# A two-layer mixture kernel on one core: routing arithmetic in fewer instructions, another split table, extra products in two gaps

## What is computed

```python
# layer 0: per-sample LoRA mixture, then a layer norm and a ternary, fake-quantised product
y = x @ W_base.T + b_base + 2.0 * einsum(x, As, Bs, cond_8)
xn = (y - mean(y)) * rsqrt(var(y) + 1e-5) * gamma + beta
xq = round(xn / s) * s,            s = max|xn| / 127        # over the whole tensor
wq = alpha * sign(w) * (|w| > d),  d = 0.7 * mean|w|, alpha = sum(|w| mask) / sum(mask)
x  = x + xq @ wq.T
# layer 1: the two best of 8 experts per sample and a shared MLP, then a 4-bit quantised FFN
w, sel = top_k(softmax(cond_8), 2);  w = w / sum(w)
c  = sum over sel of w * mlp_e(x) + mlp_shared(x)           # mlp: (gelu(x@g) * (x@u)) @ d
x  = x + ffn(c)                                             # scales are maxima over whole tensors
```

## Time and profile before

| | us |
|---|---|
| median of 3 runs (lowest, highest) | 471.18 (466.37, 471.56) |
| the profiled execution's own time | 469.8 |
| its span | 468.1 |
| end of stage one (last maximum of a chunk) | 66.5 |
| first expert product | 99.5 |

### The profile page before, as it was taken

One profiled execution on the slowest core, in us unless ns is written; L12 is line 12 of the kernel. 1 busy time (PEld: TensorE's weight loads), 2 busy tenths in 40 slices (PEclk: granted clock), 3 DMA queues, 4 the chain that ended last, 5 costly groups with the idle time before them and its releaser, 6 DMA issues.

```text
span 468.1 us, 8624 instructions
## 1 busy us (share of the span) xinstructions
PE 393.8 (84%) x2602; PEld 346.6 (74%) x2602; DVE 334.8 (72%) x571; ACT 270.3 (58%) x406; POOL 252.8 (54%) x444
## 2 busy tenths in 40 slices
PE   5998987989999999999999999999999960000697
PEld 4675855779999999999999998877767640000497
DVE  4286648857888777767777766736958899979662
ACT  3355578855454545454545454676657899568360
POOL 1266644777777666666565401555457025969230
PEclk9997999999999999999999999999999995555599
DMA  8679870058777776767777721900000000000012
GB/s 277 239 265 340 307 242 0 1 215 272 269 233 260 246 275 235 267 239 268 234 259 249 251 78 26 355 2 1 1 0 0 1 0 0 0 1 0 0 73 109
DMA packets 31651, 71.28 MB, mean 152 GB/s; under 512 B 3571, under 2 KB 19702, under 8 KB 26614
## 3 DMA queue, kind: packets, MB, share of 16 engines
q1 hardware_dynamic: 28982, 66.33, 40.6%
q0 software_dynamic: 1152, 4.19, 2.4%
q10 hardware_dynamic: 1472, 0.20, 0.3%
HBM read 55.12 MB, written 15.60 MB: 151 GB/s over the span
## 4 chain that ended last, share of the span: by engine, by line
PE 65%; DVE 15%; POOL 7%; ACT 7%; issue 2%; DMA 2%; POOLq 1%; SPq 0%; ACTq 0%; DVEq 0%
PE ps L180 47%; PE ps L758 11%; DVE S L198 9%; PE ps L761 4%; DVE G L189 3%; PE ps L177 2%; POOL U_i L192 1%; DMA wbr<-in_L_cond_W_base_dram 1%; ACT ps L186 1%; POOL t_i L192 1%; POOL Hl L189 1%; ACT xnT L186 1%; DMA wscr<-wst 1%; POOL XCh L192 1%; ACT sq L186 1%
## 5 line engine op out<-in xcount | busy, mean ns | idle before, releaser
L713 POOL CAST xg<-XT 128x64 fp32r x312 | 113.8, 411 | 56.2 <-PE ps L180 50.2
L180 PE MATMUL ps<-xg,Wr 128*128 128x256 f32 x936 | 120.1, 284 | 1.1 <-POOL xg L713 1.1
L186 ACT ACTIVATE Gb<-ps 128x512 f32<-128x512 f32 x110 | 65.8, 598 | 94.8 <-PE ps L180 94.7
L189 DVE TENSOR_TENSOR HbS<-Gb,ps 128x512 f32<-128x512 f32 x110 | 75.4, 686 | 59.0 <-PE ps L180 57.1
L180 PEld LDWEIGHTS ps<-xg,Wr 128*128 128x128 f32 x936 | 114.2, 190 | 1.5 <-POOL xg L713 1.5
L186 ACT ACTIVATE Hh<-HbS 128x512 fp32r<-128x512 f32 x110 | 69.0, 628 | 12.9 <-DVE HbS L189 12.6
L758 PE MATMUL ps<-WD,Hh 128*128 x312 | 74.3, 328 | 0.0
L761 PE MATMUL ps<-WD,Hl 128*128 x312 | 69.4, 223 | 0.0
L189 DVE TENSOR_TENSOR Hl<-HbS,Hh 128x512 fp32r<-128x512 f32 x92 | 65.8, 723 | 2.5
L761 PEld LDWEIGHTS ps<-WD,Hl 128*128 128x128 f32 x312 | 59.8, 192 | 0.0
L758 PEld LDWEIGHTS ps<-WD,Hh 128*128 128x128 f32 x312 | 59.0, 189 | 0.0
(11 more groups left out here) (187 smaller groups left out, 699.7 us busy)
## 6 DMA issues: line engine op xcount, KB each, us to landing
Wr<-wscr SPq DMA_DIRECT2D x39, 1024.0 KB, 5.0
wscr<-wst SPq DMA_DIRECT2D x16, 512.0 KB, 4.7
yscr<-Yb SPq DMA_DIRECT2D x39, 128.0 KB, 2.7
stg<-n_L_cond_skill_gate_dram SPq DMA_DIRECT2D x8, 256.0 KB, 6.2
stg<-in_L_cond_skill_up_dram SPq DMA_DIRECT2D x8, 256.0 KB, 6.5
wdr<-n_L_cond_skill_down_dram SPq DMA_DIRECT2D x8, 256.0 KB, 5.8
out_dram<-X SPq DMA_DIRECT2D x7, 256.0 KB, 2.0
X<-in_x_dram SPq DMA_DIRECT2D x3, 512.0 KB, 6.5
```

Source lines behind the costliest of these rows:

```text
L180: return lambda e: e.matmul(o_, l, r, start=start, stop=stop, skip_group_check=True)
L186: return lambda e: e.activation(o_, i_, func, **kw)
L189: return lambda e: e.tensor_tensor(o_, a, b, op)
L713: k_xg[i] = pool.do(lambda e, s=s: e.tensor_copy(xg[:, i % XR, :, T * s:T * s + T], XT[:, :, :, bass.ds(regb[i][s], 1)].rearrange("p a t o ...
```

## The change

There are three parts. In `route()`, the running sum over experts becomes one `tensor_tensor_scan`, the seven comparisons that build `etF` one wide comparison and a reduction, two multiplications one, the four index writes one, and the ternary mask with its two sums four instead of eight. That makes 9 VectorE instructions of 29; they do not leave the places in the rounds where `fill` puts them. Second, `SPLITS` takes two tiles instead of three in rounds 3 and 4, and three instead of two in rounds 6 and 7. Third, two groups of products are added whose results nobody reads: eight of `ones` by `ones` ahead of everything on TensorE, for which the memset of `ones` moves ahead of that of `identF` on POOL, and ten of `AsTh` by `xTh` in round 2, between `hidden(1)` and `rows()`.

```diff
--- before.py
+++ after.py
@@ -137,6 +137,7 @@
         bcI = at("bcI", [128, 1], I32)
         bcF = at("bcF", [128, 1], F32)
         etF = at("etF", [1, 40], F32)
+        etX = at("etX", [1, NT, E - 1], F32)
         ST = at("ST", [128, 2, 8], F32)
         KC = at("KC", [128, 8], F32)
         assert off[0] <= RH
@@ -252,8 +253,8 @@
             load_w(n)
 
 
+        k_one = pool.do(lambda e: e.memset(ones[:, :], 1.0))
         pool.do(lambda e: e.memset(identF[:, :], 0.0))
-        pool.do(lambda e: e.memset(ones[:, :], 1.0))
         k_io8 = pool.do(lambda e: e.iota(ioi[:, :], pattern=[[1, NSLOT]], base=0, channel_multiplier=0))
         k_bc = pool.do(lambda e: e.iota(bcI[:, :], pattern=[[0, 1]], base=0, channel_multiplier=1))
         k0 = pool.do(lambda e: e.memset(tri[:, :], 1.0))
@@ -339,29 +340,25 @@
             d_f = dve.do(red(S[:, 10:11], fwr[:, :], ADD, True), l_fw)
             d_ = dve.do(ts(S[:, 80:88], S[:, 80:88], RM, RM, ADD, SUB), d_)
             yield
-            d_ = dve.do(cp(S[:, 88:96], S[:, 80:88]), d_)
-            yield
-            for i in range(1, E):
-                d_ = dve.do(tt(S[:, 88 + i:89 + i], S[:, 87 + i:88 + i], S[:, 88 + i:89 + i], ADD), d_)
-                yield
+            d_ = dve.do(lambda e: e.tensor_tensor_scan(S[:, 88:96], ones[:, 0:8], S[:, 80:88], 0.0, MUL, ADD), d_, k_one)
+            yield
             d_ = dve.do(tt(S[:, 96:104], S[:, 88:96], S[:, 80:88], SUB), d_)
-            d5 = dve.do(ts(etF[:, 0:NT], iof[0:1, 0:NT], S[0:1, 88:89], None, ALU.is_ge))
+            d5 = dve.do(tt(etX[0:1, :, :], iof[0:1, 0:NT].rearrange("p (i a) -> p i a", a=1).broadcast_to([1, NT, E - 1]),
+                           S[0:1, 88:95].rearrange("p (a e) -> p a e", a=1).broadcast_to([1, NT, E - 1]), ALU.is_ge))
             yield
             d_ = dve.do(stt(S[:, 96:104], S[:, 96:104], float(SL), S[:, 72:80], MUL, ADD), d_)
+            d5 = dve.do(red(etF[:, 0:NT].rearrange("p (i a) -> p i a", a=1), etX[0:1, :, :], ADD), d5)
             yield True
             p_f = pe.do(mm(bank[6][:, 16:17], ones[:, :], S[:, 10:11], True, True), d_f)
-            for i in range(1, E - 1):
-                yield
-                d5 = dve.do(stt(etF[:, 0:NT], iof[0:1, 0:NT], S[0:1, 88 + i:89 + i], etF[:, 0:NT], ALU.is_ge, ADD), d5)
-                if i < 3:
-                    k = 48 if i == 1 else 56
-                    d_ = dve.do(tt(S[:, k:k + 8], S[:, k:k + 8], S[:, 96:104], MUL), d_)
-                if i == 3:
-                    d_ = dve.do(red(S[:, 42:44].rearrange("p (k a) -> p k a", a=1),
-                                    S[:, 48:64].rearrange("p (k e) -> p k e", k=2), ADD), d_)
-                if i == 4:
-                    for p in range(4):
-                        tok["sidx"] = dve.do(ts(sidx[:, 2 * p:2 * p + 2], S[:, 42:44], 4.0, float(p), MUL, ADD), d_)
+            yield
+            two = S[:, 48:64].rearrange("p (k e) -> p k e", k=2)
+            d_ = dve.do(tt(two, two, S[:, 96:104].rearrange("p (a e) -> p a e", a=1).broadcast_to([128, 2, E]), MUL), d_)
+            yield
+            d_ = dve.do(red(S[:, 42:44].rearrange("p (k a) -> p k a", a=1), two, ADD), d_)
+            yield
+            tok["sidx"] = dve.do(stt(sidx[:, :].rearrange("p (q k) -> p q k", k=2),
+                                     S[:, 42:44].rearrange("p (a k) -> p a k", a=1).broadcast_to([128, 4, 2]), 4.0,
+                                     iof[:, 0:4].rearrange("p (q a) -> p q a", a=1).broadcast_to([128, 4, 2]), MUL, ADD), d_)
             yield
             dve.do(ts(tmpP[:, :], iof[:, :], S[:, 42:43], None, ALU.is_equal), d_)
             dve.do(ts(etI[:, 0, 0:NT], etF[:, 0:NT], 512.0, None, MUL), d5)
@@ -372,20 +369,15 @@
             yield
             d_ = dve.do(ts(S[:, 44:45], bank[6][:, 16:17], 0.7 / 16384, None, MUL), p_f)
             yield
-            d6 = dve.do(ts(S[:, 45:46], S[:, 44:45], -1.0, None, MUL), d_)
-            dve.do(ts(tpos[:, :], fwr[:, :], S[:, 44:45], None, ALU.is_gt), d_)
-            yield
-            d_ = dve.do(ts(tneg[:, :], fwr[:, :], S[:, 45:46], None, ALU.is_lt), d6)
+            d6 = dve.do(ts(tneg[:, :], fwr[:, :], -1.0, S[:, 44:45], MUL, ALU.is_gt), d_)
+            yield
+            d_ = dve.do(stt(tpos[:, :], fwr[:, :], S[:, 44:45], tneg[:, :], ALU.is_gt, SUB), d6)
             yield True
             p_ = pe.do(mm(bank[6][0:1, 0:NSLOT], bcF[:, :], Pm[:, :], True, True), d_P)
-            d7 = dve.do(tt(tsc[:, :], tpos[:, :], tneg[:, :], ADD), d_)
-            d_ = dve.do(tt(tpos[:, :], tpos[:, :], tneg[:, :], SUB), d_)
-            yield
-            d7 = dve.do(red(S[:, 46:47], tsc[:, :], ADD), d7)
-            yield
-            d_ = dve.do(tt(tsc[:, :], tpos[:, :], fwr[:, :], MUL), d7)
-            yield
-            d_ = dve.do(red(S[:, 47:48], tsc[:, :], ADD), d_)
+            dve.do(red(S[:, 46:47], tpos[:, :], ADD, True), d_)
+            yield
+            d_ = dve.do(lambda e: e.tensor_tensor_reduce(out=tsc[:, :], in0=tpos[:, :], in1=fwr[:, :], scale=1.0, scalar=0.0,
+                                                         op0=MUL, op1=ADD, accum_out=S[:, 47:48]), d_)
             yield True
             tok["ord"] = dve.do(cp(ordI[:, :], bank[6][0:1, 0:NSLOT]), p_)
             yield True
@@ -410,6 +402,8 @@
                 if not held:
                     held = bool(next(routing, True))
 
+        for _ in range(8):
+            pe.do(mm(bank[3][:, 0:128], ones[:, :], ones[:, :], True, True), k_one, sig=False)
         fill(1)
         A0, A1, AZ, AV, AR = (bank[0], bank[1]), bank[2], bank[3], bank[4], (bank[5], bank[7])
         a_xh, d_xl, d_hs, p_h, p_z, p_v, p_r = {}, {}, {}, {}, {}, {}, {}
@@ -450,7 +444,7 @@
                 a_sq[i] = act.do(acp(sq[:, i % 2, :], AZ, ACT.Square, bias=KC[:, 5:6]), p_z[i], *opt(p_v, i - 2))
                 a_zg[i] = act.do(acp(xnT[:, cols(i)], AZ, ACT.Identity, scale=S[:, 8:9], bias=KC[:, 6:7]), p_z[i], tok["gb"])
 
-        SPLITS = (0, 2, 2, 3, 3, 2, 2, 2, 0, 3, 0, 0)
+        SPLITS = (0, 2, 2, 2, 2, 2, 3, 3, 0, 3, 0, 0)
         for n in range(12):
             i, held = n, False
             if i < 8:
@@ -472,6 +466,8 @@
                 a_be[i] = act.do(acp(xnT[:, cols(i)], xnT[:, cols(i)], ACT.Identity, bias=S[:, 9:10]), d_xn[i])
             if n == 2:
                 hidden(1)
+                for _ in range(10):
+                    pe.do(mm(AZ, AsTh[:, :], xTh[:, 0, :], True, True), sig=False)
                 rows()
             if n >= 2:
                 norm_in(n - 2)
```

## The result

The changed kernel takes 467.32 us (median of 20 runs, 465.87 to 470.16) where the kernel before takes 470.36 (20 runs, 466.07 to 472.43) beside it on the same chip. The ratio is 0.995, with a 95% interval of 0.9926 to 0.9973: a gain of 3.0 us by the medians and 2.4 by the ratio, real but about a third of the 8.7 forecast.

A forecast was written before the change was run, and what follows sets the result against it. It took TensorE's chain (65%) as the bound, slowed in stage one by the low clock before 24 us and a pause at 36. Terms 5.3 + 3.5 - 0.1 = 8.7 us off 471.18 gave 462.5, range 457.5 to 468.0.

The forecast's parts named there:

- The splits: Rounds 5 and 6: moving third tiles removes 6.0 us excess, less one 0.74 wait; net 5.3 us, bounds 0 and 6.0.
- That the clock stays high: Rounds 6 and 7: TensorE's clock stays high after the new third tiles' wait, as in round 4; no loss charged.
- the slower rival: Ten products return nothing, full transfer queue delays `sq` in rounds 6 and 7, clock falls: 475.6 us, chance 0.05.
- The ten products: Round 2: cost 2.3 us at the high clock, give back 5.8 through round 3; net 3.5, bounds -4.3 and 4.5.
- the rival in which the clock rises late: Rounds 1 to 3: the ten start low and rise on the way, gaining 0.8 instead of 3.5: 465.2 us, chance 0.20.
- The eight products: TensorE's start: they run at the low level, mostly covered by the wait for `wbr`; loss 0.1 us, at most 0.6.
- The routing at nothing: VectorE in stage one: shorter routing arithmetic hides behind other work; gain 0, bounds 0 and 1.0 us.
- The cover named: Stage one rounds: TensorE's own work in a round hides VectorE's routing operations, so their saving counts 0.
- The sum itself: Whole kernel: splits 5.3, ten products 3.5 and eight products -0.1 add to 8.7 us.
- what stage one gives or loses should pass to the end undiminished: Stage one to the end: later stages start from its results, so all 8.7 us should reach the total.
- "both": Stage one: clock rises late and transfers set the pace, 0.8 + 3.0 - 0.1 = 3.7 us gained: 467.5 us, chance 0.10.
- its transfers: Rounds 4 to 8: transfers set the pace, 2.3 us longer; ScalarE waits in each of rounds 5 to 8; 464.8, chance 0.13.

The follow-up runs named there:

- halved transfers: Changed kernel sending only the high half of each expert weight to the scratch tensor (256 KB a tile), read twice, so remainders are wrong: 467.36 us, ratio 0.9978.
- late `WQ`: Changed kernel with the three `WQ` loads issued at the end of round 8 instead of round 4: 467.02 us, ratio 0.9965.
- the even table: Changed kernel with `SPLITS` at two tiles in each of rounds 1 to 8, three in round 9: 462.12 us, ratio 0.9889.
- the even table once more: Changed kernel with two tiles in each of rounds 1 to 8, run again in another group: 462.13 us, ratio 0.9866.
- the even table alone: Kernel before with only `SPLITS` set to two tiles in each of rounds 1 to 8, old routing, no added products: 466.73 us, ratio 0.9941.

## Why the prediction was wrong

**The splits: the step that failed.** The prediction wrote "I charge one wait as in round 3, 0.74, since four buffers still stand between, and leave the clock high", and gave the term 5.3 us. In the profile, what lies behind the start of round 5 is worth 2.7, with the help of the routing, and over a dozen runs the table alone brings nothing that could be told (1.0008). The first half, that the waits of rounds 3 and 4 go and rounds 5 and 6 come near 4.8, was right to 0.5 us. The price of the third tiles was not: in place of one wait of 0.74 stand three, 2.69, 0.60 and 1.09. The row taken for it (0.74) was that of the first third tile of the kernel before, in round 3, behind a queue that had been idle (a share of 0.03); the new third tiles stand in rounds where the share is 1.03 to 1.04. The nearer rows were 1.56 and 1.33, of tiles behind a fuller queue (shares of 0.79 and 0.92); charging those makes the term 6.0 - 2.9 = 3.1. Taking out the third tiles gives 462.1, a fifth buffer with the third tiles in place 464.2, so that third tiles over four buffers are the cause is shown. Of tile 12's 2.69 us, 1.6 to 1.7 hangs on the bytes: halved transfers and late `WQ` leave 1.02 and 1.08. The rest is the round trip of a buffer. In the changed kernel the high half of tile 8 starts at 33.95, its subtraction at 36.62 (behind a power on GpSimd, which waits 1.50 for VectorE), its transfer is issued at 37.93, and tile 12 may go at 43.08: the buffer was held 9.1 us. Two tiles a round give it two rounds of 4.8, 9.6 us; tile 12, the third of its round, would have started at 40.39, 6.4 us after tile 8. A transfer 1.7 us shorter does not close that.

**That the clock stays high** held in the profile of the change. In those of the table alone, without the ten, and with `WQ` late it fell, behind pauses of 2.36, 2.39 and 2.57 us, and it fell for a shorter time behind 1.21 and 2.00 with halved transfers and without the eight. That is half of the slower rival's mechanism. It fits that the same table is worth 2.7 us in one execution and nothing in the median of the table alone; but in how many executions the clock falls was not counted, so this is argued and not shown.

**The ten products.** Forecast 3.4 with the eight, measured 2.3 up to the start of round 5. `rows()`, z, v and round 3 gave their gains. h of chunk 1 and part of the ten did not, since the level had fallen back before 10.88: 0.6 is missing for h, and 0.9 for the ten (3.24 instead of 2.3), while `rows()` gave 0.35 more than the 0.5 counted. It is half of the rival in which the clock rises late. The term was mis-sized by a premise, that the high level is there from round 1 on. The Trainium skill's rule (TensorE: Matmul & The Clock Gate, Part 4, PE-mode transpose), that transposes don't engage the full clock, is neither borne out nor refuted: the level was high at 9.07 after ten transposes and a 1.15 us wait, low at 10.88 after four and 0.44. Four transposes do run at the high level, 0.60 us (at 9.84) for 1.09 at the low; whether they raise or hold it is what stays open. With the old table the term was given back whole (0.9992); with the even table it stands, at 2.6 us for the ten; and in the change, too, the gain by the ratios goes with them (1.0013 without).

**The eight products.** Forecast -0.1. They delay `w2r` by 0.3 (4.64 for 4.33), inside the bound of 0.6; in the profile of the change h of chunk 0 is then at the high level, and without them at the low one, where the ten take 2.88. But with the eight, the even table and the old routing h of chunk 0 is at the low level too (0.57 and 0.43 apart at 8.93). No worth of their own could be told.

**The routing at nothing** had only bounds and no price, and is the second step that failed. Alone the medians agree (469.98 against 469.67), but rounds 5 and 6 are 1.8 us shorter with it in the profile, and with the even table it is worth 1.6. The cover named, TensorE's own work in a round, did not hold in round 6, where VectorE was busy for the whole 5.86 us. The sentence that explained away VectorE's 7.46 busy of 8.39 us in round 5 as "time in which GpSimd works too" named the mechanism and drew no price from it. The Trainium skill says that the two share a port pair under an exclusive lock, held for a whole instruction, which a VectorE instruction with two SBUF inputs contends for with a GpSimd one that reads SBUF (SBUF — State Buffer, section "SBUF: two separate sides"). The trace agrees: 0.28 alone, 1.35 and 1.37 beside subtractions of 1.28, and 0.15 and 1.28 for the small one.

**The sum itself.** The three parts alone show no gain in their medians beyond 1.2 us, together they bring 3.0 us, with the even table 7.5. They are not terms of a sum: what a part gains ahead of the transfers is paid back at the next wait, as the products alone show (round 5 starts 1.4 us earlier, and takes 9.07), until the wait itself is removed. And that "what stage one gives or loses should pass to the end undiminished" held only in part: 5.0 us became 3.4. Of the rivals, "both" came out closest, at 467.5 against 467.32, and that is luck: its transfers were the right suspect, but the sign it was to show ("in each of rounds 5 to 8") was not there, since only tiles of rounds 6 and 7 wait.

**Left open**: the 0.8 us in stage two, where the clock fell in this execution and, in the same place, in three others (five buffers, the even table once more, and the routing with the eight); and the 1.3 before 304 us. And the four to five us of spread between runs of one kernel are of the size of what the clock does in stage one (round 2 took 7.8 us with the table alone and 12.6 with the even table, the routing and the eight, both without the ten). Run by run, time and mean granted clock go together in some kernels: the even table once more has its five runs of 459.7 to 460.5 at mean granted clocks of 0.932 to 0.937, and its four of 463.6 to 463.9 at 0.926; without the ten the three near 464.8 are at 0.926 and the four from 469.5 on at 0.916 to 0.919. With the even table alone no such order is seen; its profile has a granted clock of 1.00 in rounds 2 and 3 although the products start 0.43 apart there. What decides the level was not found.

## What to carry to other kernels

When work is spread over rounds, look first at how many buffers stand between the producer and the transfer it waits on, and price a moved piece by the wait of a row whose queue is as full as it will be there, not by the first wait of the series. Test parts together with the limit removed as well as each alone: three parts of which none showed a clear gain alone gave 0.5% together, and 1.3% once an even table, 0.6% by itself, took the last waits away. And a short vector instruction with two SBUF inputs beside a GpSimd instruction that reads SBUF is to be priced by the latter's duration, as the 1.28 to 1.37 us here beside 1.28.

## What the runs showed of the hardware

- The granted clock and the pauses of TensorE before v. Behind 2.26 us, 2.36, 2.39, 2.57 and 2.65, the eight records of v last 1.56 to 1.87 and the clock stays low for over 6 us. Behind 1.00 and 1.68 in the changed kernel, and 1.87 with the table alone (at 44.03), v lasts 1.05 and nothing falls. Behind 1.21 (halved transfers), 1.80 (routing alone) and 2.00 (without the eight), v lasts 1.05 as well, but the clock goes down about 2 us after v starts, for over 3 us. So from 1.2 to 2.0 us the length of the pause alone does not tell whether the clock falls.
- The level in round 2 differs between kernels whose TensorE work up to there is the same. With the table alone z of chunk 0 ran at the high level (starts 0.23 apart at 15.67), and round 2 took 7.8 us against 11.19 before, although no product had been added.
- A transfer to the scratch tensor of 512 KB takes 5.0 us from issue to landing while the share is 1.0 (10 of them, 30 to 60 us, with the change). One of 256 KB takes 3.8 (10 of them, the same stretch, with halved transfers). That of tile 8, 5.15 us, is over half of the 9.1 us for which its buffer is held.
- VectorE beside GpSimd, with two SBUF inputs: 1.28 us for 128x8 and 1.35 to 1.37 for 128x128 while a GpSimd subtraction of 1.28 runs, 0.15 and 0.28 when GpSimd is idle (the even table with the old routing).
